# Batch 0 taken through residual and second norm before batch 1 is rounded, in a gated cross-attention and mixture-of-experts block

## The reference, cut to what matters

```python
# x: (4, 256, 256); ctx: (4, 256, 256)
def attention(x, weight):                    # one product per batch
    xq = quant_dequant_act_1x128(x)          # fp8 rounding, one scale per row and 128 columns
    wq = quant_dequant_weight_128x128(weight)
    return jnp.einsum('emk,enk->emn', xq, wq)

x = x + jnp.tanh(g_xattn[0]) * attention(_layernorm(x), ctx_2048)
x = x + jnp.tanh(g_ffn[0]) * ffn(_layernorm(x), ...)

def ffn(x, ...):                             # 1024 tokens of width 256
    # softmax over 8 experts, the best 4 kept; each expert is silu(x wg) * (x wu) then wd, 176 wide,
    # plus a shared expert, 704 wide, times a sigmoid gate
    return moe_out + sgate * shared
```

## Time and profile before

| | us |
|---|---|
| median of 3 runs | 190.42 |
| lowest, highest | 189.87, 191.33 |
| the profiled execution | 189.87 |
| its span | 188.1 |

### The profile page before, as it was taken

One profiled execution on the slowest core, in us unless ns is written; L12 is line 12 of the kernel. 1 busy time (PEld: TensorE's weight loads), 2 busy tenths in 40 slices (PEclk: granted clock), 3 DMA queues, 4 the chain that ended last, 5 costly groups with the idle time before them and its releaser, 6 DMA issues.

```text
span 188.1 us, 2346 instructions
## 1 busy us (share of the span) xinstructions
PE 163.8 (87%) x747; PEld 124.8 (66%) x755; DVE 127.6 (68%) x273; ACT 103.8 (55%) x231; POOL 90.8 (48%) x95
## 2 busy tenths in 40 slices
PE   0122798999959999999999999999999999999993
PEld 0010357878737777777777787887777777777761
DVE  1888974989997779998965424988347544544453
ACT  2499462976528986547485564445754444444330
POOL 6120612664543254847668426544645555856310
PEclk9999999999999999999999999999999999999999
DMA  4999991000000000000000000200000000000002
GB/s 140 271 375 356 334 348 49 2 0 0 0 0 3 0 0 2 2 0 3 0 0 2 0 3 0 112 0 0 0 0 0 3 2 0 0 0 3 0 0 112
DMA packets 4368, 9.97 MB, mean 53 GB/s; under 512 B 617, under 2 KB 617, under 8 KB 4356
## 3 DMA queue, kind: packets, MB, share of 16 engines
q1 hardware_dynamic: 4356, 9.83, 15.3%
HBM read 8.78 MB, written 1.05 MB: 52 GB/s over the span
## 4 chain that ended last, share of the span: by engine, by line
PE 71%; DVE 16%; ACT 7%; issue 2%; DMA 2%; DVEq 0%
PE bank L943 62%; DVE a_lo L736 3%; PE bank L901 2%; PE bank L996 2%; DVE act L725 2%; DMA x<-xs 2%; ACT xc L360 1%; PE bank L982 1%; ACT cw L352 1%; DVE comb_parts L714 1%; DVE x L643 1%; PE bank L987 1%; PE bank L983 1%; DVE up L698 1%; ACT xc L343 1%
## 5 line engine op out<-in xcount | busy, mean ns | idle before, releaser
L296 POOL TENSOR_TENSOR gu_lo<-w_raw,gu_hi 128x512 fp32r<-128x512 f32 (+1 forms) x34 | 49.2, 1447 | 26.6 <-ACT gu_hi L426 18.6
L943 PE MATMUL bank<-h_hi,gu_hi 128*128 128x512 f32 x124 | 52.8, 425 | 0.0
L303 POOL TENSOR_TENSOR d_lo<-w_raw,d_hi 128x256 fp32r<-128x256 f32 (+1 forms) x34 | 27.3, 804 | 49.3 <-ACT d_hi L431 49.2
L725 DVE TENSOR_TENSOR act<-silu,bank 128x512 f32<-128x512 f32 (+1 forms) x34 | 23.3, 686 | 40.3 <-PE bank L943 37.7
L440 ACT ACTIVATE silu<-bank 128x512 f32<-128x512 f32 (+1 forms) x34 | 20.3, 596 | 51.9 <-PE bank L943 50.3
L943 PE MATMUL bank<-h_hi,gu_lo 128*128 128x512 f32 x124 | 48.5, 391 | 0.0
L943 PE MATMUL bank<-h_lo,gu_hi 128*128 128x512 f32 x124 | 48.3, 389 | 0.0
L943 PE MATMUL bank<-a_hi,d_hi 128*128 128x512 f32 (+1 forms) x68 | 28.5, 419 | 0.5 <-DVE a_lo L736 0.4
L736 DVE TENSOR_TENSOR a_lo<-act,a_hi 128x512 fp32r<-128x512 f32 (+1 forms) x34 | 26.1, 768 | 1.1 <-ACT a_hi L448 0.7
L943 PEld LDWEIGHTS bank<-h_hi,gu_lo 128*128 128x128 f32 x124 | 23.3, 188 | 5.3
L943 PE MATMUL bank<-a_hi,d_lo 128*128 128x512 f32 (+1 forms) x68 | 26.7, 392 | 0.0
(11 more groups left out here) (117 smaller groups left out, 185.1 us busy)
## 6 DMA issues: line engine op xcount, KB each, us to landing
w_raw<-w_full SPq DMA_DIRECT2D x16, 384.0 KB, 4.7
x<-xs SPq DMA_DIRECT2D x4, 256.0 KB, 6.8
cw<-ctx_t SPq DMA_DIRECT2D x4, 256.0 KB, 6.0
out_t<-fin SPq DMA_DIRECT2D x4, 256.0 KB, 2.1
w_raw<-w_last SPq DMA_DIRECT2D x1, 256.0 KB, 6.8
spread<-sel SPq DMA_DIRECT2D x1, 111.4 KB
small_in<-small SPq DMA_DIRECT2D x1, 11.0 KB, 6.4
```

The source lines that it names most:

```text
L296: nc.gpsimd.tensor_tensor(gu_lo[:, slot, 0:cols], w_raw[:, c, 0:cols], gu_hi[:, slot, 0:cols].bitcast(F32), ALU.subtract).then_inc(gu_lo_d ...
L303: nc.gpsimd.tensor_tensor(d_lo[0:rows, slot, :], w_raw[0:rows, c, at:at + D], d_hi[0:rows, slot, :].bitcast(F32), ALU.subtract).then_inc(d ...
L725: nc.vector.tensor_tensor(act[0:rows, slot, :], silu[0:rows, slot, :], up, ALU.mult).then_inc(gated_done, 1)
L943: last = nc.tensor.matmul(out, w[k][a], x_of[k][b], start=(start and k == 0 and i == 0), stop=(stop and k == blocks - 1 and i == 2))
```

## The change: what it does

Batch 0's whole way through the residual and the statistics of the second norm now stands ahead of batch 1's rounding on VectorE. In batches 0 and 1 both halves of the attention are added by VectorE (`residual_both`): four instructions for half 1, a wait for them, four for half 0. ScalarE's `residual0` and VectorE's `residual_sum` are gone for these two batches; batches 2 and 3 stay as they were. ScalarE takes x of batch 1 ahead of the context of batch 1, and `norm_x1(0)` moves ahead of `high_gu(1)`. GpSimd's `low_gu(0)` waits for `deq_ready` in place of `xq_ready`, and `low_gu(1)` comes after the first `inverse_std` of the second norm. On TensorE, `attend(1)` moves behind the seven clock matmuls and behind `transpose_y2(0)`, where it takes the place of the two other clock matmuls.

```diff
@@ gpsimd @@
+            pool.wait_ge(deq_ready, 1)
+            low_gu(0)
+            inverse_std(1, 0, var1_ready, rstd1_ready)
             pool.wait_ge(xq_ready, 2)
-            low_gu(0)
-            pool.wait_ge(x1_ready[0], 1)
             low_gu(1)
-            inverse_std(1, 0, var1_ready, rstd1_ready)
@@ scalar @@
+            scale_x(1)
+            mags_x(1)
             scale_ctx(1)
             mags_ctx(1)
-            scale_x(1)
-            mags_x(1)
-            residual0(0)
+            copy_xqt(1)
+            norm_x1(0)
             high_gu(1)
-            copy_xqt(1)
-            residual0(1)
@@ vector @@
+            def residual_both(b):
+                v.wait_ge(att_ready, b + 1)
+                v.wait_ge(deq_ready, b // HB + 1)
+                for k in (1, 0):
+                    for jj, j in enumerate(tiles(b)):
+                        for n in range(2):
+                            ns = slice(n * P, (n + 1) * P)
+                            last = nc.vector.scalar_tensor_tensor(x[:, j, ns], ATT[b][k][:, jj * D + n * P:jj * D + (n + 1) * P],
+                                                                  deq[:, j, k, n:n + 1], x[:, j, ns], ALU.mult, ALU.add)
+                    if k == 1:
+                        last.then_inc(res1_ready, 1)
+                        v.wait_ge(res1_ready, b + 1)
+                    else:
+                        last.then_inc(res0_ready, 1)
@@ vector, order @@
+            residual_both(0)
+            stats_x1(0)
+            lifted = lift_x(1)
+            round_x(1, lifted)
+            shift_x1(0)
             lifted = lift_ctx(1)
             round_ctx(1, lifted)
-            lifted = lift_x(1)
-            round_x(1, lifted)
-            residual1(0)
-            residual_sum(0)
-            stats_x1(0)
-            residual1(1)
-            shift_x1(0)
-            residual_sum(1)
+            residual_both(1)
             stats_x1(1)
@@ tensor @@
             transpose_xq(1)
-            attend(1)
             keep_clock_up(7)
             transpose_y2(0)
-            keep_clock_up(2)
+            attend(1)
             gate_up_first(0, 0)
```

More of the change, by code:

```diff
@@ L470, in _ @@
                 .then_inc(gate_hi_done, 1)
-            norm_x1(0)
             high_h(0)
@@ L654, in stats_x1 @@
             def stats_x1(b):
-                v.wait_ge(x1_ready[b], 1)
+                if b < HB:
+                    v.wait_ge(res0_ready, b + 1)
+                else:
+                    v.wait_ge(x1_ready[b], 1)
                 stats(1, b, moments(1, b)).then_inc(var1_ready, 1)
@@ L905, in transpose_x1 @@
                 if b == 0:
-                    pe.wait_ge(x1_ready[1], 1)
+                    pe.wait_ge(res0_ready, 2)
                 else:
```

## The result

| | before | changed |
|---|---|---|
| median, us | 190.63 (4 runs) | 194.51 (4 runs) |
| lowest to highest | 189.87 to 191.33 | 194.07 to 195.14 |
| mean granted clock of TensorE | 1.0 in the profiled run | 0.982, 0.991, 0.991, 0.982 |

The ratio is 1.020, with a 95% interval of 1.0157 to 1.0242. The interval is clear of 1. The time lies in the range; the forecast of 193.3 is 1.2 us short. The clocks stand in the order of the runs: 194.72 and 195.14 had 0.982, 194.31 and 194.07 had 0.991. The profiled execution took 194.72 against 189.87, 4.85 us more.

What follows compares the result with a forecast made beforehand. TensorE and VectorE were taken to hang on batch 1's start on TensorE at 30.84. A 2.92 us delay on 189.87 gave 192.8 for the profiled execution, 193.3 us on the median; range 191.6 to 196.1.

Steps and rivals of the forecast that it cites:

- step 1: Batch 0's residual on VectorE: eight instructions take 2.30 us, from 15.93 to 18.23.
- step 2: VectorE's statistics, then rounding x of batch 1: rounded x ready at 20.80, 1.71 us late.
- step 3: TensorE up to batch 0's transposes: clock matmuls end at 24.28; batch 0's normed rows ready at 23.1, against 24.57 before.
- step 4: TensorE's moved attend(1) ends at 26.23, 4.75 us late; VectorE stands from 22.2 to 26.27.
- step 5: VectorE's low_h(0) queues behind batch 1's residual and statistics; TensorE's matmuls on h_lo start at 30.47, 2.92 us late.
- Step 6: TensorE then proceeds as before: batch 1's transposes at 32.39, its normed rows ready at 31.98, its work at 33.76.
- the clock rose during the clock matmuls: Rival: TensorE's clock rises during the seven clock matmuls, delay 1.3 us, total 191.7 us; chance 0.06.
- the fallen clock: Rival: TensorE's clock falls in the new pause of 3.2 us before h_lo, giving 196.1 us; chance 0.11.
- The forecast's own sign of being wrong: TensorE matmuls after 30.5 keeping a pace of 0.21 us per 256 columns in place of 0.12.
- The price of 2.8 us: Loss if TensorE's clock falls in the new pause: some 5.7 us of work at half pace.
- The collisions of VectorE with GpSimd: Rival: fewer VectorE and GpSimd collisions after the shift; 191.6 us with L714 alone, chance 0.05; a gain, chance 0.04.
- Nothing hid the delay: Rival: delay hidden, if VectorE were not bound by TensorE at 39.07; within the chance of 0.06.

Runs made afterwards that it cites:

- experiment 1: Changed kernel with attend(1) put back right behind transpose_xq(1), ahead of the seven clock matmuls; 191.54 us, ratio 1.0041 to the kernel before.
- experiment 3: Changed kernel with low_h(0) on VectorE moved ahead of batch 1's residual and statistics; 195.01 us, ratio 1.0223 to the kernel before.
- e2: Changed kernel with 12 more clock matmuls filling TensorE's pause before batch 0's matmuls on h_lo; 192.79 us, ratio 1.0103 to the kernel before.
- b0: The kernel before, unchanged, run again for a trace of the low-clock group; 191.42 us, clock 0.991.
- b1: The kernel before with 10 clock matmuls filling TensorE's 2.25 us router pause; 189.63 us, ratio 0.9952 to the kernel before.
- experiment 4: Changed kernel with 11 clock matmuls before transpose_xq(1) in place of seven behind it, attend(1) ahead of transpose_y2(0); 191.35 us, ratio 1.0037 to the kernel before.

## Why the prediction was right and where it was wrong

*Steps 1 and 2 were right, and of step 3 the norm of batch 0.* The eight additions took 2.32 until the statistics (2.30 forecast). Rounded x of batch 1 came 1.73 late (21.31 - 19.15 - 0.43; 1.71). Batch 0's normed rows were ready at 23.53, which is 23.1 and the 0.43 of the loads.

*Steps 4 and 5 had the right mechanism, with the wait too long.* `attend(1)` stood behind matmuls that nobody waited for, VectorE idled before it, `h_lo` was queued behind it, and TensorE paused. Experiments 1 and 3 show the root. VectorE idled 2.79 us (about 4 forecast), TensorE 2.72 (some 3). The delay was 1.68 for 2.92 in the profiled execution, because the clock rose during the clock matmuls (2.66 us from their first start to the transposes, 2.99 at the low pace) and the transposes and the attention ran at full pace; the case was among the rivals, with a delay of 1.3 and a chance of 0.06. `e2`, whose clock rose later, shows 2.66 (30.21 - 27.55, its first attention at 14.86 as before).

*Step 6 was right*: no wait for batch 1's rows.

*The step that failed is the reading of the earlier trace rows*, that 2.25 us of pause do no harm, and with it the chance of 0.11 for the fallen clock; the forecast itself had the clock stay up. The forecast's own sign of being wrong is in the trace: behind the pause the starts are 0.22 apart for 256 columns, not 0.12. In all four runs of the changed kernel the granted clock was 0.982 or 0.991, so it fell in each. In the profiled one it fell behind the new pause; which pause it was in the two runs of 0.991 (some 3.5 us at half pace) no trace shows, since the router's pause is there too. The price of 2.8 us came out at 2.76, and `e2` shows the full pace when the pause is filled; that it fits so closely is luck, since it was worked out for 5.7 us at half pace and the clock stayed low for 6.9, part of which TensorE spent waiting. The reading rested on one execution; by `b0` and `b1` this very pause makes the clock fall in more than half of the runs. So a longer pause was no step into the unknown, but one beyond a pause that already failed.

The Trainium skill ("TensorE: Matmul & The Clock Gate", "Why this matters for your kernels") says in its table that an idle gap between bursts of matmuls brings the array back to its low clock. The trace agrees in kind, with a granted clock of 0.51 over 6.9 us behind the pause; the page warns of gaps somewhat longer than those of 2.72 and 2.25 us that sufficed here, and the measurement decides.

So two rivals came together, an earlier rise and a fall: 192.8 forecast for the profiled execution, - 1.24 (1.68 for 2.92), + 2.76, + 0.43 for the loads, is 194.75 against 194.72 measured. The two errors, 1.24 too much and 2.76 left out, have opposite signs, so it is in part luck that the forecast of the median missed by only 1.2 us.

*The other rivals.* The collisions of VectorE with GpSimd stayed as they were (1.89 and 1.90 us for the cast), as argued. Nothing hid the delay.

## What to carry to other kernels

A matrix product whose result is at the head of another engine's chain must not stand behind filler matmuls or behind work whose consumer has slack; look for the engine that would stand idle meanwhile. Where a schedule opens a pause on TensorE, price the pause and the work behind it at half pace, and read the granted clock of every run before calling a pause harmless, since one trace shows one of two cases. Compare kernels at like clocks: medians over both groups can hide a loss, as in experiment 1. Filling the router's pause alone (189.63, 0.5% under the kernel before) was worth as much here as any reordering tried with its pauses filled (189.82, 190.14 and 190.27).

## What the runs showed of the hardware

In 18 of 29 executions of one kernel the granted clock was 0.988 to 0.991, in 11 it was 1.0; with its pause of 2.25 us filled it was 0.999 or 1.0 in all 12. In the one fall that was traced the matmuls ran at 1.2 GHz for some 3.4 us, 0.43 us each in place of 0.23. The groups differ by 1.1 us on the whole (191.1 against 190.0, the medians). In experiment 4 the clock fell with no pause longer than 1.05 us, after 4 us in which TensorE was busy for 2.16. At the start of an execution the pace is the low one while the column of the granted clock shows 1.00 (kernel before, 20 to 25 us): there only the distance of the starts tells the clock.

Runs at a clock of 1.0 differ too, and the traces show one reason: the first load of x took 3.28 us in the first trace of the kernel before, 3.67 in the second, 3.71 in the changed kernel and 4.12 in `b1`, and the first attention followed at 14.87, 15.26, 15.30 and 15.70. So a load that lands late moves the start of the chain by up to 0.8 us between executions of nearly the same program.
